# Seams around a quantised feed-forward: weight steps, halves, order of roundings, and when rows are loaded

## The reference

```python
x = x + tanh(g_xattn[0]) * _L0_xattn_ref(_layernorm(x), ctx, ctx, mask, ...)
x = x + tanh(g_ffn[0])   * _L0_ffn_ref(_layernorm(x), w_gate, w_up, w_down)
x = x + tanh(g_xattn[1]) * _L1_xattn_ref(...)
x = x + tanh(g_ffn[1])   * _L1_ffn_ref(...)

def _L0_ffn_ref(x, w_gate, w_up, w_down):          # H = 256, I = 768
    x = act_qdq(x)                                 # 16 bits, one scale for all of x
    up = act_qdq(x @ lpbq_dequant(w_up).T)         # weights: 4 bits, a scale for each 32
    gate = act_qdq(x @ lpbq_dequant(w_gate).T)
    sig = fixed_qdq_u16(jax.nn.sigmoid(gate))
    gate = act_qdq(gate * sig)
    o = act_qdq(gate * up)
    return o @ lpbq_dequant(w_down).T
```

## Time and profile before

| what | value |
|---|---|
| median of 3 runs | 1316.18 us (1313.89 to 1317.72) |
| the profiled execution | 1312.19 us |
| span of its trace | 1310.9 us |
| busy PE, DVE, ACT, POOL | 94%, 68%, 54%, 37% |
| mean granted clock of PE | 0.982 |
| attention of layer 0, about | until 471 us |
| gate, up and silu, product, down | from 483.5, 550.2, 621.8, 693.9 us |
| end of the down stage | 768 us |

### The profile page before, as it was taken

How to read it: one execution, slowest core, us unless ns; L and a number is a source line. 1 busy time by engine, 2 the same in 40 slices (tenths; PEclk the granted TensorE clock), 3 DMA queues, 4 the chain that set the end, 5 groups by cost and what they waited for, 6 DMA issues and landing times.

```text
span 1310.9 us, 25392 instructions
## 1 busy us (share of the span) xinstructions
PE 1231.4 (94%) x9385; PEld 872.9 (67%) x9385; DVE 895.8 (68%) x2671; ACT 711.0 (54%) x1192; POOL 479.6 (37%) x675
## 2 busy tenths in 40 slices
PE   6799999999999989999999988999999999889998
PEld 5467776766667654445458865677676676578987
DVE  2678777777777656599897946777867867542333
ACT  1355555555555539888863325666566566522221
POOL 5344443344332100166000324344543643322555
PEclk7899999999999999999999998999999999999999
DMA  5523334333232050000004633446465342137973
GB/s 156 146 71 97 108 97 111 89 100 109 83 110 59 18 170 0 1 1 1 0 1 138 185 116 106 123 131 159 125 170 132 114 125 73 50 136 220 313 204 39
DMA packets 121941, 137.23 MB, mean 105 GB/s; under 512 B 12881, under 2 KB 116427, under 8 KB 121797
## 3 DMA queue, kind: packets, MB, share of 16 engines
q1 hardware_dynamic: 112176, 126.25, 32.5%
q0 software_dynamic: 7296, 8.15, 3.4%
q10 hardware_dynamic: 2346, 1.22, 0.3%
HBM read 58.42 MB, written 27.36 MB: 65 GB/s over the span
## 4 chain that ended last, share of the span: by engine, by line
PE 52%; DVE 9%; issue 5%; ACT 3%; POOL 2%; DMA 1%; ACTq 0%; SPq 0%; POOLq 0%; DVEq 0%
PE PS L574 10%; PE PS L380 5%; PE PS L619 5%; PE PS L320 5%; PE PS L363 4%; PE PS L339 4%; PE PS L587 4%; PE PS L412 3%; PE PS L438 2%; PE PS L628 2%; PE PS L327 2%; DVE AM L1261 2%; DVE NM L989 1%; DVE G L1268 1%; PE PS L421 1%
## 5 line engine op out<-in xcount | busy, mean ns | idle before, releaser
L733 ACT ACTIVATE P<-PS 128x512 f32<-128x512 f32 x512 | 302.3, 601 | 165.1 <-PE PS L366 94.5
L986 DVE CUSTOM_DVE_ANT_0 MX<-PS,NQ 128x256 bf16<-128x256 f32 x512 | 192.7, 418 | 68.0 <-PE PS L339 67.7
L363 PE MATMUL PS<-QS,KS 99*128 99x256 bf16 x1024 | 227.3, 276 | 9.1 <-ACT P L733 8.1
L989 DVE TENSOR_REDUCE NM<-PS 128x2 f32<-128x512 f32 x256 | 173.8, 686 | 71.2 <-PE PS L339 69.2
L339 PE MATMUL PS<-KS,QS 96*128 96x256 bf16 x1024 | 198.6, 276 | 21.0 <-DVE NM L986 11.7
L339 PEld LDWEIGHTS PS<-KS,QS 96*128 96x128 bf16 x1024 | 87.4, 98 | 88.0 <-issue 25.5
L380 PE MATMUL PS<-P,V 128*32 128x256 f32 x2048 | 139.4, 390 | 1.7 <-ACT P L733 1.7
L363 PEld LDWEIGHTS PS<-QS,KS 99*128 99x128 bf16 x1024 | 95.2, 99 | 55.5 <-ACT P L733 23.2
L366 PE MATMUL PS<-NK,identb 128*128 128x256 bf16 x512 | 127.4, 274 | 0.0
L574 PE MATMUL PS<-XNT,wup 128*128 128x512 f16 x576 | 124.8, 379 | 0.0
L574 PEld LDWEIGHTS PS<-XNT,wup 128*128 128x128 f16 x576 | 56.2, 98 | 67.5
(11 more groups left out here) (232 smaller groups left out, 2458.7 us busy)
## 6 DMA issues: line engine op xcount, KB each, us to landing
KS<-PP SPq DMA_DIRECT2D x192, 128.0 KB, 2.9
QS<-PP SPq DMA_DIRECT2D x192, 128.0 KB, 2.4
WH<-in_wex SPq DMA_DIRECT2D x16, 768.0 KB, 7.5
WG<-in_wex SPq DMA_DIRECT2D x10, 768.0 KB, 5.1
bufd<-bias_row SPq DMA_DIRECT2D x5, 1032.0 KB, 11.0
XE<-bufd SPq DMA_DIRECT2D x32, 129.0 KB
XB<-in_x SPq DMA_DIRECT2D x16, 256.0 KB, 3.0
CT<-in_ctxT SPq DMA_DIRECT2D x16, 256.0 KB, 3.3
```

Source lines behind the costliest of these rows:

```text
L363: ins = tensor.matmul(o, t.KS[b % 3][0:99, h, 128 * kt:128 * kt + 128], t.QS[b % 3][0:99, h, :], start=True, stop=(L == 1))
L733: scalar.activation(t.P[h % 8][:, :, :], PS[:, h % 2, :].rearrange("p (k n) -> p k n", k=2), ACT.Exp).then_inc(s_ex, 1)
L986: ins = vector.tensor_tensor_reduce(t.MX[:, 2 * (h % 2) + qt, :], PS[:, bk, 256 * qt:256 * qt + 256], t.NQ[b % 4][:, qt, :], -1.0, 1.0e30, ...
L989: ins = vector.tensor_reduce(nm[:, :, h], PS[:, bk, :].rearrange("p (t n) -> p t n", t=2), X, ALU.max, negate=True)
```

## The change

It does the following, from the top of the diff:

- `wq_step`: steps run in slots k = 0, 3, 5, 8, 11, 13 instead of every third slot. The condition is the same in `pe_slot`, `act_slot`, `dve_slot`, `pool_slot` and `sp_slot`; it is shown for the first two.
- `pe_ff_in` waits for the lower part of its own 512 columns, half by half; in `dve_ffn` the second integers come after the first lower part.
- `pe_down` waits for the lower part by tt; block 0's quantising, upper and lower part are done in halves of 128 columns (`half_of`), so the counts of s_dq, s_dh and s_dl go up by one.
- `early_slots` returns a table: slot (-3, 0) at block 1, slot (-3, 1) at block 3, the rest as before.
- one more up chunk is made between the two halves of scale 2; the warm-ups are 13, 0, 11, 18 and 11 instead of 17, 7, 14, 36 and 23.
- ACT issues a sigmoid of one column ahead of the sigmoids, and in the product stage rounds silu c ahead of up c (before: silu c, then up c + 2).

```diff
--- before.py
+++ after.py
@@ -512,15 +512,17 @@
                     if s - 2 == NB - 1:
                         pe_warm(5, 10)
                     pe_ranks(GROUP_OF[s - 2][0])
-            if L == 0 and s >= 0 and (16 * s + k) % 3 == 0 and wq_step(s, k) < 3 * WQ:
+            if L == 0 and wq_step(s, k) in range(3 * WQ):
                 pe_weights(*divmod(wq_step(s, k), WQ))
         WQ = 33
         WNAMES = (("wup", wup, 2), ("wgate", wgt, 2), ("wdown", wdn, 6))
         def wq_step(s, k):
-            return (16 * s + k) // 3
+            return 3 * ((16 * s + k) // 8) + (0, 3, 5).index(k % 8) if s >= 0 and k % 8 in (0, 3, 5) else -1
         def wq_part(i, j):
...
@@ -559,8 +561,6 @@
         def pe_ff_in(w, i):
             c = i % NCH
-            if i < NCH:
-                pe.wait_ge(s_xl, 2 * (c // 6) + 2)
             if 3 <= i < NCH + 3:
                 pe.wait_ge(s_fa, i - 2)
             elif NCH + 3 <= i < 2 * NCH + 3:
...
@@ -569,6 +569,8 @@
                 pe.wait_ge(s_uq, i - 2 - 2 * NCH)
             for half in range(2):
                 n, mt = 2 * (c // 6) + half, c % 6
+                if i < NCH:
+                    pe.wait_ge(s_xl, n + 1)
                 for j, (wp, xp) in enumerate(PARTS * 2):
                     k = j // 3
                     ins = tensor.matmul(PS[:, 2 * (i % 3) + half, :], w[:, wp, k, 128 * mt:128 * mt + 128],
...
@@ -578,9 +580,10 @@
         def pe_down(b):
             bk = b % 6
-            pe.wait_ge(s_dl, b + 1)
+            pe.wait_ge(s_dl, b + 2 if b else 1)
             pe.wait_ge(s_x2, b - 5)
             for tt in range(2):
+                pe.wait_ge(s_dl, b + tt + 1)
                 for j, (wp, xp) in enumerate(((0, 0), (1, 0), (0, 1)) * 6):
                     k = j // 3
                     c = 512 * b + 256 * xp + 128 * tt
...
@@ -645,7 +648,9 @@
         def early_slots():
-            return list(slots(1))[:20]
+            first = list(slots(1))[:20]
+            return {1: first[:1], 3: first[1:2], **{b: first[2 * b - 6:2 * b - 4] for b in range(4, 13)}}
         def late_slots():
             return list(slots(1))[20:]
...
@@ -659,7 +664,7 @@
             pe.wait_ge(s_am, NB)
             pe_scale_a(0)
             pe_scale_b(0)
-            pe_warm(5, 17)
+            pe_warm(5, 13)
             for i in range(NCH):
                 pe_ff_in(wgt, i)
             pe_ff_in(wup, NCH)
...
@@ -670,23 +675,22 @@
             pe_ff_in(wup, 2 * NCH)
             pe_ff_in(wup, 2 * NCH + 1)
             pe_scale_a(2)
-            pe_warm(6, 7)
+            pe_ff_in(wup, 2 * NCH + 2)
             pe_scale_b(2)
-            pe_warm(6, 14)
+            pe_warm(6, 11)
             pe_scale_a(3)
             pe_scale_b(3)
-            for i in range(2 * NCH + 2, 3 * NCH):
+            for i in range(2 * NCH + 3, 3 * NCH):
                 pe_ff_in(wup, i)
-            pe_warm(6, 36)
+            pe_warm(6, 18)
             pe_scale_a(4)
             pe_scale_b(4)
-            pe_warm(6, 23)
+            pe_warm(6, 11)
             early = early_slots()
             for b in range(NB):
                 pe_down(b)
-                if 3 <= b < 13:
-                    for s, k in early[2 * b - 6:2 * b - 4]:
-                        pe_slot(1, s, k)
+                for s, k in early.get(b, ()):
+                    pe_slot(1, s, k)
             pe.wait_ge(s_x2, NB)
             for s, k in late_slots():
                 pe_slot(1, s, k)
...
@@ -849,8 +853,13 @@
                     act_logits(s - 2)
                 if L == 1 and k == 7 and GROUP_OF[s - 2][1] == GROUP_OF[s - 2][2] - 1:
                     act_route(GROUP_OF[s - 2][0])
-            if L == 0 and s >= 0 and (16 * s + k) % 3 == 0 and wq_step(s, k) < 3 * WQ:
+            if L == 0 and wq_step(s, k) in range(3 * WQ):
                 act_weights(*divmod(wq_step(s, k), WQ))
+        def half_of(half):
+            return slice(0, 256) if half is None else slice(128 * half, 128 * half + 128)
         def banks(i):
             return PS[:, 2 * (i % 3):2 * (i % 3) + 2, :].rearrange("p k n -> p (k n)")
...
@@ -906,9 +915,10 @@
             act.wait_ge(s_gu, c - 3)
             scalar.activation(VQ[c % 4], chunk(c), ACT.Copy, scale=col(S4 + 2)).then_inc(s_vq, 1)
-        def act_down_in(b):
-            act.wait_ge(s_dq, b + 1)
-            scalar.activation(GH[:, :, 512 * b:512 * b + 256], OQ[b % 2], ACT.Copy).then_inc(s_dh, 1)
+        def act_down_in(b, half=None):
+            t = half_of(half)
+            act.wait_ge(s_dq, b + 1 + (half != 0))
+            scalar.activation(GH[:, :, 512 * b:512 * b + 256][:, :, t], OQ[b % 2][:, :, t], ACT.Copy).then_inc(s_dh, 1)
         def act_turn(e):
             q, j = divmod(e, 4)
...
@@ -941,6 +951,8 @@
                 if c:
                     act_sign(c - 1)
             act_sign(NCH - 1)
+            scalar.activation(gates[:, 1:2], gates[:, 0:1], ACT.Sigmoid)
             for c in range(NCH):
                 act_sigmoid(c)
                 if c + 1 < NCH and by_act(c + 1):
...
@@ -950,17 +962,17 @@
             act_up_int(1)
             for c in range(NCH):
                 act_silu_int(c)
-                if c + 2 < NCH:
-                    act_up_int(c + 2)
+                if c >= 2:
+                    act_up_int(c)
             early = early_slots()
-            act_down_in(0)
+            act_down_in(0, 0)
+            act_down_in(0, 1)
             act_down_in(1)
             for b in range(NB):
                 if b + 2 < NB:
                     act_down_in(b + 2)
-                if 3 <= b < 13:
-                    for s, k in early[2 * b - 6:2 * b - 4]:
-                        act_slot(1, s, k)
+                for s, k in early.get(b, ()):
+                    act_slot(1, s, k)
             act.wait_ge(s_x2, NB)
             act_ones(1)
             for s, k in late_slots():
...
@@ -1279,18 +1291,26 @@
             vector.tensor_scalar(chunk(c), chunk(c), 1.0, None, ALU.mult, ALU.min,
                                  accum_out=AM[:, 24 + c:25 + c]).then_inc(*dve.tick())
-        def dve_down_quant(b):
-            t = slice(256 * b, 256 * b + 256)
-            dve.wait_ge(s_dl, b - 1)
-            vector.scalar_tensor_tensor(OQ[b % 2], G[:, :, t], col(S5 + 2), SGN[:, :, t], ALU.mult, ALU.mult).then_inc(s_dq, 1)
+        def dve_down_quant(b, half=None):
+            t, own = slice(256 * b, 256 * b + 256), half_of(half)
+            if b >= 2:
+                dve.wait_ge(s_dl, b)
+            vector.scalar_tensor_tensor(OQ[b % 2][:, :, own], G[:, :, t][:, :, own], col(S5 + 2), SGN[:, :, t][:, :, own],
+                                        ALU.mult, ALU.mult).then_inc(s_dq, 1)
+        def dve_down_low(b, half=None):
+            t = half_of(half)
+            dve.wait_ge(s_dh, b + 1 + (half != 0))
+            if half == 0:
+                dve.wait_ge(s_dq, 2)
+            vector.tensor_tensor(GH[:, :, 512 * b + 256:512 * b + 512][:, :, t], OQ[b % 2][:, :, t],
+                                 GH[:, :, 512 * b:512 * b + 256][:, :, t], ALU.subtract).then_inc(s_dl, 1)
         def dve_down_in(b):
             if b + 1 < NB:
                 dve_down_quant(b + 1)
-            dve.wait_ge(s_dh, b + 1)
-            vector.tensor_tensor(GH[:, :, 512 * b + 256:512 * b + 512], OQ[b % 2],
-                                 GH[:, :, 512 * b:512 * b + 256], ALU.subtract).then_inc(s_dl, 1)
+            dve_down_low(b)
         def dve_ffn():
             dve.wait_ge(s_wl, 18)
...
@@ -1301,10 +1321,10 @@
             dve_scale_b(0)
             dve_scale_c(0)
             dve_x_int(0)
-            dve_x_int(1)
             vector.tensor_tensor(col(US), col(S1), wsc[:, 0, 2:3], ALU.mult)
             vector.tensor_tensor(col(GS), col(S1), wsc[:, 1, 2:3], ALU.mult).then_inc(s_us, 1)
             dve_x_low(0)
+            dve_x_int(1)
             dve_x_low(1)
             for c in range(NCH):
                 dve_gate_max(c)
...
@@ -1346,14 +1366,18 @@
             dve_scale_b(4)
             dve_scale_c(4)
             early = early_slots()
-            dve_down_quant(0)
+            dve_down_quant(0, 0)
+            dve_down_quant(0, 1)
+            dve_down_low(0, 0)
+            dve_down_quant(1)
+            dve_down_low(0, 1)
             vector.tensor_scalar(col(FS), col(S5), col(S4), col(S2), ALU.mult, ALU.mult).then_inc(*dve.tick())
             dve.wait_ge(*dve.last())
             vector.tensor_scalar(col(FS), col(FS), tg[:, 2:3], 1.0 / 65536.0, ALU.mult, ALU.mult).then_inc(*dve.tick())
             dve.wait_ge(*dve.last())
             vector.tensor_tensor(col(FS), col(FS), wsc[:, 2, 2:3], ALU.mult).then_inc(*dve.tick())
-            dve_down_in(0)
-            dve_down_in(1)
+            dve_down_low(1)
+            dve_down_quant(2)
             dve.wait_ge(*dve.last())
             for b in range(NB):
                 if b + 2 < NB:
...
@@ -1362,9 +1386,8 @@
                 dve.wait_ge(d_xd[b % 3], 16 * uses(0, b, 3))
```

(15 more changed lines are left out.)

6 lines of the change are left out of this document (3 added, 3 removed).

## The result

The changed kernel takes 1307.87 us (median of 6 runs, 1305.18 to 1309.8) beside 1317.38 for the kernel before on the same chip (6 runs, 1313.89 to 1321.08): a ratio of 0.9943, interval 0.9925 to 0.9961. It is faster, by 0.4 to 0.75%. The ratio is the recorded estimate from the runs; the two medians alone would give 0.9928. I had forecast 13.6 us, 1.03%; the interval says 5 to 10 us. On the median that the forecast started from, 1316.18, the ratio gives 1308.7 us, where I had 1302.6 and a range of 1298 to 1308.5. Between the two profiled executions it is 4.7 us (span 1310.9 to 1306.2). So the sign held; by the ratio nearly half of the gain is missing, by the profiles two thirds.

A forecast was written before the change was run, and what follows sets the result against it. It took the attention as bound by TensorE instructions and the feed-forward seams by latency chains; -3.4 + 0.3 + 0 - 6.0 - 1.9 - 2.6 = -13.6 us, from a median of 1316.18 to 1302.6, range 1298 to 1308.5.

The forecast's parts named there:

- Part 1: Attention of layer 0 and the seam behind it: denser weight steps, -5.5 + 1.3 + 0.8 = -3.4 us.
- The seam: Between attention and first scale transpose: without wdown's transposes there, PE starts 5.5 us sooner.
- the tail: Last heads of the attention: the step in slot 259 puts a transposing pair ahead of them, +0.8 us.
- the term for the steps inside the attention: PE-bound attention blocks: six transposing steps added, +1.3 us; fixed phase kept near zero, bound -1 to +6.
- Rival (c): Attention: it pays +4 to +6 us for the dense steps instead of +1.3, total 1305 to 1308; chance 0.12.
- Rival (d): Attention: steps with DVE work make PE wait 0.7 us each, 20 more hits eat the gain, 1320; chance 0.03.
- Part 2: Gate's start: first chunk in halves, PE starts earlier but then idles, +0.3 us.
- Part 3: Ahead of the first real sigmoid: the table load is hidden already, zero; the skill's figure would give up to 2.7 us.
- Part 4: Product stage: one chunk moved ahead (2.6 us) and ScalarE's new order, together -6.0 us.
- Part 5: Start of the down stage: first batch in halves, -2.6 + 0.7 = -1.9 us.
- Part 6: Down stage: layer 1's first rows loaded at block 1 instead of 3, removing PE's waits for remainders, -2.6 us.
- Rival (a): Gate's start or down stage: the clock falls, 2.6 to 5.2 us more, 1305 to 1308; chance 0.12.

The follow-up runs named there:

- e7: Changed kernel with layer 1's slot (-2, 11), four TensorE transposes and ScalarE's copy, moved from behind block 12 to behind block 13; ratio to the kernel before 0.9913.
- e6: Changed kernel with one of the 99 weight steps (wup's step 20) moved from slot 5 to slot 4 of the third heads' queue; ratio to the kernel before 0.9929.
- e5: Changed kernel with the dense weight steps at slots 0, 3, 4 of every eight instead of 0, 3, 5; ratio to the kernel before 0.9899.
- e4: Changed kernel with the gate's start (order of first integers, waits, 17 warm-ups) as in the kernel before; ratio to the kernel before 0.9928.
- e8: Changed kernel with ScalarE's old order in the product stage, the additional chunk ahead kept; ratio to the kernel before 0.9968.
- e11: Changed kernel with the first down batch whole again instead of in halves; ratio to the kernel before 0.9948.
- e1: Changed kernel with the weight steps back at every third slot; ratio to the kernel before 0.9912.
- e3: Changed kernel with slot (-3, 0), the load of layer 1's first rows, back at block 3; ratio to the kernel before 0.9937.
- e10: Changed kernel with the old weight steps (one in three) and slot (-2, 11)'s transposes behind block 13; 1299.17 us, ratio to the kernel before 0.9906.
- e2: Kernel before with only the weight steps moved to slots 0, 3, 5 modulo 8; ratio to the kernel before 0.9995.
- e9: Changed kernel with weight steps at 0, 3, 4 of eight and slot (-2, 11)'s transposes behind block 13; 1298.36 us, ratio to the kernel before 0.9887.

## Why the prediction was right and where it was wrong

**Part 1, denser weight steps: the step that failed.** The seam was right (-4.97 for -5.5), and so was the tail: with slot 259 the last block takes 12.9 us for 11.9, +1.0 for +0.8. What failed is the term for the steps inside the attention: +1.3, with the phase held "near zero for it, as the blocks of the earlier trace rows have such steps too". Two things are wrong in it.

First, the block from 331.13 to 358.76 us was read as holding six transposing steps, and it holds three. The other three stand in the block behind it, which took 27.6 us too. PE in order of time, the kernel before:

```profile
344.28 0.44 PE L547 MATMUL PS<-ident,w_nat 128*128 128x128 f32 x2
...
353.52 0.38 PE L547 MATMUL PS<-ident,w_nat 128*128 128x128 f32 x2
...
360.59 0.38 PE L547 MATMUL PS<-ident,w_nat 128*128 128x128 f32 x2
...
370.09 0.38 PE L547 MATMUL PS<-ident,w_nat 128*128 128x128 f32 x2
```

By the same working, six steps are +2.9 and not +1.4. Second, the blocks of the earlier trace rows hold a single step that quantises on VectorE (at 314.2 us), so they could not tell what such steps cost at other places. That term was put at nothing, and it is the larger error.

What the runs showed in its place: between first out and the last XM the dense steps cost 8.2 us, where I had 2.1. By blocks, from one output projection to the next, the first five, in which wup's steps stand, are 5.6 us longer than before; the next six, with wgate's, 0.5 shorter; the last four 3.1 longer, and only 1.0 of that is in the last two, where the moved transposes of wdown stand. So most of it is paid where no work was added. Taken apart by kernels, the 8.2 are 1.6 for one step at a bad place (e7 against e6), 1.1 for the clock that fell behind it, 3.0 for the places of the others (e6 against e5, without the 1.8 that the clock took at e5's last output projection), and 2.5 that are left in e5 (1.2 and 4.3, if that fall of the clock belongs to e5's places). These 2.5 are near the 2.1 of the working, and yet no proof of it: with six steps counted right it gives 3.6. Which single waits make up the 3.0 and the 2.5 was not taken apart. The 6.1 us that are missing lie at the edge of the stated bound of 6, nine steps with 0.7, and for a different reason: many small losses, and one of 1.8.

**Rival (c)** was thus the right one for the attention. It was held at 0.12, with +4 to +6 for the term of 1.3, and was itself too small: 8.2 less 1.0 for the tail is 7.2. The prediction's own mark for being wrong, "if the attention ended over 3 us later", came true: 7.2 us later.

**Rival (d)** had the mechanism (a step lets PE wait for maxima, at the place where DVE divides heads) and not the size: three waits more than before, not 20.

**Part 2, gate in halves:** +0.23 for +0.3, shown by e4 alone.

**Part 3, sigmoid first:** nothing, as said.

**Part 4, product:** -6.02 for -6.0, and e8 splits it into 2.59 and 3.43 for 2.6 and 3.4. The working by instructions of a chain that is bound by two engines in turn came out at every point.

**Part 5, first down batch in halves:** -2.44 + 0.70 = -1.74 for -2.6 + 0.7 = -1.9 (e11).

**Part 6, rows sooner: right in size and wrong in what comes next.** In e1, e5 and e6 the stage takes 72.16 us; the working gives 74.24 + 0.7 - 2.6 = 72.3. That it came out so near is in part luck: by e3 the rows' stall would have cost 5.8 us without this part, not 2.6. In the changed kernel's own profile the stage took 75.01. The step that failed is "What is late next is DVE at blocks 10 to 12, as now". It named the place but took its price as fixed at the 1.1 us of before, which was a wait for ScalarE. It isn't fixed: once VectorE is the later one, the wait grows with when x1 rows land, and goes from 1.1 to 4.5 us over the kernels, with the clock falling behind the longer ones. A stall at the end of a chain of DMAs is no constant that cancels.

**Rival (a), the clock,** was looked for at the wrong places. It did not fall at the gate nor in the idle bits of 1.0 us at both seams (granted clock 1.00 from 480 to 490 and from 674 to 690 us). It fell behind waits of PE of 1.8 and 2.65 us in the middle of busy stretches. Where the seam was left as it was (e1, e10) it cost 2.7 us around it. The Trainium skill ("TensorE: Matmul & The Clock Gate", HAM oscillation) tells of a kernel whose matmuls wait for a DMA at each tile and fall back to the low clock each time. The trace agrees for 144 to 148 us of the changed kernel, though the wait there is for VectorE; it does not for each time, since in e7 the same wait of 1.77 us leaves the clock at 1.00.

**The sum.** The parts add to -13.6, the profile shows -5.25 at the values: 6.1 missing in the attention, 0.5 at its seam, 2.7 down, less 1.0 of an earlier first out. The parts worked out from rows of the same instructions (2, 3, 4, 5) are off by 0.3 us together. The two with a term for which no row of before stood (1 and 6) are off by 9, partly for the 2.2 us of clock that fell behind the two new waits.

## What to carry to other kernels

Before work is moved into the slots of a busy stage, write out the in-order queue of each engine that it passes through, at each slot where it will stand: what counts is less how much it adds than whether that engine is idle there before the bounding engine needs it next. One step of 99 cost 1.6 us more than the same step one slot sooner. Count the steps that a reference block really holds before you take a price from it. And where a stall hangs on a DMA, place the consumer so that its engine has a block of other work ahead; the place of four transposes was worth 0.6 to 6.4 us and made the stage repeat to 0.01 us.

## What the runs showed of the hardware

After a wait of 1.77 us of TensorE, in a stretch in which it is otherwise nearly always busy, the granted clock fell to 0.50 for some 4 us in three kernels (changed, e2, e3) and stayed at 1.00 in four others (e4, e7, e8, e11) with the same instructions and the same wait. The same eight output matmuls at the end of the attention took 1.99 us (before) or 3.60 us (e1, e10) with the same code around them. In the 4 us ahead of them TensorE was busy 1.72 us in the changed kernel (468 to 472), where the clock stayed at 1.00, and 2.12 us in e9 (462 to 466), where it fell. Two VectorE instructions took 1.96 us beside GpSimd instructions and 1.1 without. Apart from that the traces repeat closely: stages without a fall of the clock and without a DMA at their end agree to 0.1 us between kernels, which is what made differences of 0.2 us readable where the times of one kernel scatter by 2 to 10.
